# A transformer decoder layer on one core: new order of the opening, and stack rows interleaved over the partitions

## The chip, the cores and the metric

The kernel runs on one core of a Trainium2 chip. The metric is the device time of one execution in microseconds (us).

## The reference

One decoder layer over x of 4 × 512 tokens with 256 numbers each, and a context of 4 × 1024 tokens:

```
x = layernorm(x + attention(x, x, causal))      # 16 heads of 16, scores / sqrt(16), softmax
x = layernorm(x + attention(x, context))        # the same, not causal
x = layernorm(x + moe(x))                       # 8 experts 256 -> 1024 -> 256, gelu, the best 2 of each token
```

Each attention has projections wq, wk, wv, wo of 256 × 256 with biases. All inputs and the output are float32.

## The kernel before, in words

The kernel has two parts. The first (to about 855 us) does both attentions, the norms and the routing; the second does the experts on the tokens sorted by expert, and the last norm. The change touches the first.

**Splits and stacks.** Scores are computed in bf16, yet nearly as exactly as in float32: a projected query or key is split into three bf16 pieces, and the contraction of 16 numbers becomes one of 96: `Q_PART` and `K_PART` say which piece of the query meets which piece of the key in each of six groups of 16 rows. Three further rows hold the row maxima (in three pieces) on the query's side and ones on the key's. One "split" (b, s) makes the pieces for 8 heads and 512 tokens: PE projects (L899, two 512-wide float32 matmuls), ACT writes `rest` and the first piece (L1038, L1039), POOL the second and third (L807 to L811), and SP issues six DMAs (L737) from `parts` (128 partitions, d by h) into the stack (16 rows for each group, 8 heads). Per batch there are ten: 0, 1 queries and 2, 3 keys of the self attention, 4 to 7 keys of the cross attention, 8, 9 its queries. There are two `parts` buffers: ACT starts a split only once the one before last has landed. The self stacks share memory with the experts' weights and are named `stack_or_weights` in the profile; the others are `q_stack_cross` and `k_stack_cross`.

**Units.** A unit is four heads of one batch in one attention: 8 units for the self attentions of batches 0 and 1, then cross and self units in turn. For a unit, "max" multiplies queries by keys on PE (L929, L933, with a mask L934) and DVE reduces the rows (L1101); POOL splits the maxima (L821 to L827), PE turns them (L940), DVE copies them (L1108), and SP writes them to the query stack (L745, `rows_in`). "score" multiplies again with keys as rows (L956, mask L959), ACT takes exp (L1059), "weigh" multiplies by the values (L971). `values` (L912, L1047) are projected in pairs of token tiles. Then come turning and dividing (`o_turn`), `att_turn`, `out`, `stats` and `norm`.

**Order.** `Planner` (L89) simulates the engines with rough costs and writes one list, `ORDER`, at build time. Each engine walks through that list, doing its share in order, with semaphores between the engines; so an instruction that waits holds up all of its engine's later ones. `begin` (L176) puts the loads and constants first and sets the times from which the plan starts.

**The opening before.** SP issues three weights and six bias columns (L704 to L707) under one semaphore, `first_in`, which PE, ACT and DVE each wait for ahead of everything. Then it issues five weights, the router's, two output biases, six norm rows and the router's bias under `const_in`; the projections from the context, the first `out` and the `more_constants` of DVE and POOL wait for all 15. POOL issues x, context and residual (L762 to L772), makes masks, identity and ones (L774 to L800), and waits for `const_in`, before its first split.

Of the kernel before, what the change touches and what calls it, by code (L numbers as in the profile page):

```python
# [75 lines left out]
def key_tiles(kind):  # L76
    return ET if kind else QT
# [8 lines left out]

class Planner:  # L89
# [96 lines left out]
    def needs(self, ev):  # L186
        k, d = ev[0], self.done
        if k == "split":
# [10 lines left out]
            if src is None:  # L199
                return None  # L200
# [84 lines left out]
    def place(self, ev, ready):  # L285
        k, d = ev[0], self.done
        self.order.append(ev)
        if k == "split":
# [6 lines left out]
            done = self.use("pool", high + self.HOP, 2900)  # L295
# [38 lines left out]
        elif k == "weigh":  # L334
# [34 lines left out]
        elif k == "norm":  # L369
            self.held["mv"] = None  # L370
            end = self.use("dve", ready, 1500)
            d["scaled", ev[1], ev[2]] = self.use("pool", end + self.HOP, 4800)
# [121 lines left out]
def decoder_layer(nc, a, out):  # L494
    ctx = ExitStack()
    with ctx:
# [28 lines left out]
        ln_gb = sb("ln_gb", [P, 6, D])  # L525
# [4 lines left out]
        router_b = sb("router_b", [P, E])  # L530
# [7 lines left out]
        first_in = sem("first_in")  # L538
        const_in = sem("const_in")
        const_made = sem("const_made")  # L540
        const_cast = sem("const_cast")
        w_in = [sem("w_in0"), sem("w_in1")]
# [32 lines left out]
        bias = {n: sba("b_" + n, [P, DC]) for n in ("sa_bq", "sa_bk", "sa_bv", "ca_bq", "ca_bk", "ca_bv")}  # L575
        out_b = sba("out_b", [P, 2, D])
# [26 lines left out]
        FIRST_LOADS = 3 + 6  # L603
        N_LOADS = 5 + 1 + 2 + 6 + 1
# [27 lines left out]
        ONE_PAIR = float.fromhex("0x1.007f000000000p+0")  # L632

# [60 lines left out]
        def on_vector(b, kind):  # L694
            return b == B - 1 and kind == 1

        CASTS = 8
# [4 lines left out]
        def _(sp):  # L702
            for n in ("sa_wq", "sa_wk", "sa_wv"):
                sp.dma_start(w[n][:, :, :], a[n].rearrange("(c p) n -> p c n", p=P)).then_inc(first_in, 16)  # L704
            with nc.allow_non_contiguous_dma(reason="six columns of 256 numbers"):
                for n, t in bias.items():
                    sp.dma_start(t[:, :], a[n].rearrange("(c p) -> p c", p=P)).then_inc(first_in, 16)  # L707
# [896 lines left out]
```

## Time and profile before

| | us |
|---|---|
| median of 3 runs | 1187.5 |
| lowest and highest run | 1185.99, 1188.43 |
| the profiled execution | 1185.79 |
| its span in the trace | 1183.9 |

Mean granted TensorE clock of the profiled execution: 0.938 of full speed. The span is the time from the first to the last instruction; the execution adds 1.9 us around it. Busy times of PE (matmul) and PEld (weight load) overlap. "Idle before" is the time in which an engine waited ahead of an instruction, with what released it.

### The profile page before, as it was taken

How to read it: one execution, taken by the hardware profiler on the slowest of the kernel's cores; microseconds unless marked ns; L12 is line 12 of the kernel's file. 1: busy time of each engine (PE TensorE's matmuls, PEld its weight loads, DVE VectorE, ACT ScalarE, POOL GpSimd, SP SyncE). 2: the span in 40 equal slices, each digit the busy share in tenths (PEclk: the TensorE clock that was granted, in tenths of full speed). 3: DMA queues.
4: the chain of work that ended last, by engine and by line, in shares of the span. 5: the costliest groups of instructions: out<-in, count | busy, mean ns of one | idle time of the engine just before them, and what ended most of it. 6: DMA issues, size and time to landing. Idle time of an engine off the chain costs nothing. (4 is left out here: it accounts for less than half of the span.)

```text
span 1183.9 us, 19018 instructions
## 1 busy us (share of the span) xinstructions
PE 1041.1 (88%) x6318; PEld 597.6 (50%) x6319; DVE 558.8 (47%) x905; ACT 588.9 (50%) x1199; POOL 306.5 (26%) x416
## 2 busy tenths in 40 slices
PE   3889889999999998998998998975429999999976
PEld 1544445333335533343432333321329999999965
DVE  2441467775665576665674754740321121111116
ACT  1246344675764575765565665654143334444422
POOL 5533532404105603003223030243021111111104
PEclk8989889999999999999999998996759999999988
DMA  7985466208209304107507042011031203323324
GB/s 191 130 125 81 69 78 75 43 2 100 37 2 132 57 2 62 20 2 105 154 1 81 1 55 27 1 55 54 30 101 53 98 27 111 106 102 115 107 86 141
DMA packets 71069, 83.41 MB, mean 70 GB/s; under 512 B 10592, under 2 KB 64608, under 8 KB 70880
## 3 DMA queue, kind: packets, MB, share of 16 engines
q1 hardware_dynamic: 63328, 63.17, 30.9%
q0 software_dynamic: 5504, 17.34, 4.6%
q10 hardware_dynamic: 2176, 2.10, 0.5%
q8 instruction: 37, 0.61, 0.2%
q14 instruction: 24, 0.20, 0.1%
HBM read 38.63 MB, written 12.10 MB: 43 GB/s over the span
## 5 line engine op out<-in xcount | busy, mean ns | idle before, releaser
L1101 DVE TENSOR_REDUCE max_q<-v_slot 128x1 f32<-128x1024 f32 (+3 forms) x352 | 399.7, 1172 | 185.0 <-PE v_slot L929 121.5
L1059 ACT ACTIVATE probs<-a_bank 128x512 f32<-128x512 f32 (+1 forms) x688 | 362.6, 591 | 219.8 <-PE a_bank L956 139.8
L956 PE MATMUL a_bank<-q_stack_cross,k_stack_cross 99*128 99x512 bf16 x512 | 172.9, 399 | 26.8 <-issue 11.7
L929 PE MATMUL v_slot<-k_stack_cross,q_stack_cross 96*128 96x512 bf16 x512 | 155.7, 390 | 10.0 <-DMA q_stack_cross<-parts 8.8
L1441 ACT ACTIVATE hidden<-a_bank,b 128x128 f32<-128x128 f32 x216 | 79.4, 368 | 153.2 <-PE a_bank L1389 139.2
L971 PE MATMUL o_bank<-probs,v_cross 128*32 128x512 f32 x1024 | 141.9, 627 | 9.2 <-issue 3.8
L956 PEld LDWEIGHTS a_bank<-q_stack_cross,k_stack_cross 99*128 99x128 bf16 x512 | 47.4, 99 | 167.4 <-ACT probs L1059 86.9
L1397 PE MATMUL v_slot<-stack_or_weights,hidden 128*128 128x256 f32 x576 | 130.3, 379 | 0.0
L1397 PEld LDWEIGHTS v_slot<-stack_or_weights,hidden 128*128 128x128 f32 x576 | 106.7, 190 | 13.0
L1389 PE MATMUL a_bank<-x_col,stack_or_weights 128*128 128x128 f32 x864 | 109.6, 277 | 1.6 <-issue 1.6
L1389 PEld LDWEIGHTS a_bank<-x_col,stack_or_weights 128*128 128x128 f32 x864 | 106.3, 194 | 3.8 <-issue 2.0
L1352 POOL DMA_INDIRECT token_out<-y_row,to_i x36 | 34.5, 959 | 241.7 <-DVE y_row L1534 241.7
L821 POOL CAST max_p<-max_q 128x16 bf16<-128x16 f32 x32 | 6.3, 196 | 344.0 <-DVE max_q L1101 343.9
L929 PEld LDWEIGHTS v_slot<-k_stack_cross,q_stack_cross 96*128 96x128 bf16 x512 | 43.9, 100 | 89.8 <-issue 31.7
L807 POOL TENSOR_TENSOR rest<-rest,parts 128x512 f32<-128x512 f32 x40 | 46.2, 1154 | 114.8 <-ACT parts L1039 114.5
L933 PE MATMUL v_slot<-stack_or_weights 96*128 96x128 bf16 (+3 forms) x256 | 62.9, 318 | 8.3 <-issue 4.0
L956 PE MATMUL a_bank<-stack_or_weights 99*128 99x512 bf16 (+3 forms) x256 | 66.5, 317 | 4.2 <-DMA stack_or_weights<-max_t 3.6
L1505 DVE COPY x_col<-v_slot 128x256 f32<-128x256 f32 x37 | 15.7, 424 | 114.0 <-PE v_slot L1376 114.0
L934 PE MATMUL v_slot<-mask_q,ident_b 128*128 128x128 bf16 x256 | 50.9, 228 | 0.0
L959 PE MATMUL a_bank<-mask_k,ident_b 128*128 128x128 bf16 x256 | 50.1, 225 | 0.0
L971 PEld LDWEIGHTS o_bank<-probs,v_cross 128*32 128x32 f32 x1024 | 20.7, 110 | 57.1 <-ACT probs L1059 39.4
L1120 DVE RECIPROCAL recip<-v_slot 128x16 f32<-128x16 f32 x32 | 8.2, 257 | 83.9 <-PE v_slot L979 81.9
(217 smaller groups left out, 1186.1 us busy)
## 6 DMA issues: line engine op xcount, KB each, us to landing
stack_or_weights<-in_e_w SPq DMA_DIRECT2D x16, 1024.0 KB, 7.8
stack_or_weights<-parts SPq DMA_DIRECT2D x96, 128.0 KB, 5.9
k_stack_cross<-parts SPq DMA_DIRECT2D x96, 128.0 KB, 5.9
q_stack_cross<-parts SPq DMA_DIRECT2D x48, 128.0 KB, 6.4
x_slots<-slots_in SPq DMA_DIRECT2D x38, 129.0 KB
ctxt<-in_ctxT POOLq DMA_DIRECT2D x4, 1024.0 KB, 10.6
xt<-in_xT POOLq DMA_DIRECT2D x4, 512.0 KB, 6.8
xres<-in_x POOLq DMA_DIRECT2D x4, 512.0 KB, 4.4
```

Of the source, the lines that this page charges most:

```text
L807: nc.gpsimd.tensor_tensor(rest[i][:, :], rest[i][:, :], parts[i][:, 0, :], ALU.subtract).then_inc(rest_done, 1)
L929: last = nc.tensor.matmul(slot[:, half * S:(half + 1) * S], lhs, k_stack[1][0:KR, G * u + j, half * S:(half + 1) * S], start=True, stop=True)
L933: nc.tensor.matmul(slot[:, at:at + keys], lhs, k_stack[0][0:KR, G * u + j, 0:keys], start=True, stop=False)
L934: last = nc.tensor.matmul(slot[:, at + keys - P:at + keys], ident_b[:, :], mask_q[:, :], start=False, stop=True)
L956: last = nc.tensor.matmul(bank[:, i * cols:(i + 1) * cols], lhs, q_stack[kind][0:KM, G * u + j, q0:S], start=True, stop=bool(kind))
L959: last = nc.tensor.matmul(bank[:, i * cols:i * cols + P], ident_b[:, :], mask_k[:, :], start=False, stop=True)
L971: last = nc.tensor.matmul(o_bank[32 * j:32 * (j + 1), q0:S], v_ext[kind][:, kt, G * u + j, :], probs[NO.tile[n, kt] % 2][:, j, q0:S], star ...
L1059: nc.scalar.activation(probs[tile % 2][:, js[0]:js[-1] + 1, q0:S], a_bank[at % AS][:, 0:len(js) * (S - q0)].rearrange("p (j t) -> p j t", ...
L1101: nc.vector.tensor_reduce(most, rows, X, ALU.max, negate=True).then_inc(v_free, 1)
L1389: last = nc.tensor.matmul(h_bank[f % HB][:, 0:P], w1[i][:, c, f * P:(f + 1) * P], x_col[:, c, :], start=(c == 0), stop=(c == DC - 1))
L1397: last = nc.tensor.matmul(y_bank[:, 0:D], hidden[:, f, :], w2[i][:, f, :], start=(f == 0), stop=(f == FC - 1))
L1441: nc.scalar.activation(hidden[:, f, :], h_bank[f % HB][:, 0:P], ACT.Gelu, bias=b1[:, bass.ds(e * FC + f, 1)]).then_inc(gelu_done, 1)
```

## The change

Seven edits go together:

- x of batch 0 is issued by ACT's queue, each weight gets a semaphore of its own, the six bias columns become one array laid out on the host, and the nine broadcast rows (norms, output biases, router bias) become one DMA. PE, ACT and DVE no longer wait for everything.
- POOL's order at the start becomes constants, context, residual. The constants of the routing and the adding of the residual bias of batch 0 move behind the first unit.
- The ones rows of the cross keys come by one DMA from a small memset of DVE; DVE also makes the ones and zeros of the cross values. ACT has an Exp of one column first.
- The four self splits of batch 0 are made on DVE.
- The first norm (batch 0, self) is made wholly on DVE.
- The planner does not place cross-key splits of batch 0 before the rows of unit 2 are in, and starts its clocks at 6 us.
- Stack rows are interleaved: group g takes rows g, g + 6, g + 12, ... instead of 16 g to 16 g + 15.

```diff
+def on_vector_split(b, s):
+    return b == 0 and s < 4
+def on_vector(b, kind):
+    return (b, kind) in ((0, 0), (B - 1, 1))
...
-        for ev in (("load_x", 0), ("load_ctx", 0), ("load_res", 0), ("constants",), ("more_constants",), ("add_bias", 0)):
+        for ev in (("load_x", 0), ("constants",), ("load_ctx", 0), ("load_res", 0)):
...
-        self.done["load_x", 0], self.done["load_ctx", 0], self.done["load_res", 0] = 12000.0, 16000.0, 18000.0
-        self.free["pe"] = 12000.0
-        self.free["act"] = self.free["dve"] = 13000.0
+        self.done["load_x", 0], self.done["load_ctx", 0], self.done["load_res", 0] = 6000.0, 14000.0, 16000.0
+        self.free["pe"] = self.free["act"] = self.free["dve"] = 6000.0
...
-            if src is None:
+            if src is None or (b == 0 and 4 <= s < 8 and ("rows_in", 2) not in d):
                 return None
...
+            if on_vector_split(*ev[1:]):
+                done = self.use("dve", high + self.HOP, 1800)
+            else:
+                done = self.use("pool", high + self.HOP, 2900)
...
+            if (n, kt) == (0, QT - 1):
+                self.order += [("more_constants",), ("add_bias", 0)]
...
+            if on_vector(*ev[1:]):
+                d["scaled", ev[1], ev[2]] = self.use("dve", 0.0, 2700)
...
+        ONES = 2048
+        ones_wide = probs[1][0:PARTS, :, :].rearrange("p j t -> p (j t)")[:, 0:ONES // 2].bitcast(BF16)
...
         def _(sp):
+            sp.dma_start(w["sa_wq"][:, :, :], a["sa_wq"].rearrange("(c p) n -> p c n", p=P)).then_inc(weight_in["sa_wq"], 16)
+            sp.dma_start(biases[:, :], a["biases"]).then_inc(biases_in, 16)
+            for n in ("sa_wk", "sa_wv", "ca_wk", "ca_wv"):
+                sp.dma_start(w[n][:, :, :], a[n].rearrange("(c p) n -> p c n", p=P)).then_inc(weight_in[n], 16)
+            sp.wait_ge(ones_made, 1)
+            sp.dma_start(k_stack[1][KR:KM, :, :].rearrange("p h t -> p (h t)").rearrange("p (c t) -> p c t", t=ONES),
+                         ones_wide[:, :].unsqueeze(1).to_broadcast([PARTS, H * SE // ONES, ONES])).then_inc(ones_in, 16)
+            sp.dma_start(rows_b[:, :], a["rows"].to_broadcast([P, 8 * D + E])).then_inc(rows_b_in, 16)
+            for n in ("sa_wo", "ca_wq", "ca_wo", "router_w"):
+                target = router_w if n == "router_w" else w[n]
+                sp.dma_start(target[:, :, :], a[n].rearrange("(c p) n -> p c n", p=P)).then_inc(weight_in[n], 16)
...
-                                sp.dma_start(stack[g * HD:(g + 1) * HD, h0:h0 + 8, t0:t0 + S], parts[no % 2][:, part, :]).then_inc(stack_in[s], 16)
+                                sp.dma_start(stack[g:KR:NG, h0:h0 + 8, t0:t0 + S], parts[no % 2][:, part, :]).then_inc(stack_in[s], 16)
...
                 elif k == "more_constants":
-                    pool.wait_ge(const_made, 12)
-                    nc.gpsimd.memset(ones_rows(k_stack[1]), ONE_PAIR).then_inc(const_made, 1)
-                    pool.wait_ge(const_made, 13)
-                    nc.gpsimd.memset(v_ext[1][:, :, :, HD:HD + 1], 1.0).then_inc(const_made, 1)
-                    nc.gpsimd.memset(v_ext[1][:, :, :, HD + 1:], 0.0).then_inc(const_made, 1)
-                    pool.wait_ge(const_in, 16 * N_LOADS)
-                elif k == "split":
+                    pool.wait_ge(rows_b_in, 16)
+                elif k == "split" and not on_vector_split(*ev[1:]):
...
+                    pool.wait_ge(split_done, no)
...
         def _(sc):
-            sc.wait_ge(first_in, 16 * FIRST_LOADS)
+            sc.dma_start(xt[:, :, :], xt_d[:, :, 0:S]).then_inc(xt_first, 16)
+            sc.wait_ge(biases_in, 16)
+            nc.scalar.activation(warm[:, :], biases[:, 0:1], ACT.Exp).then_inc(warmed_up, 1)
...
+                    if js[0] == 0 and tile == 1:
+                        sc.wait_ge(ones_in, 16)
...
         def _(dve):
-            dve.wait_ge(first_in, 16 * FIRST_LOADS)
...
                 elif k == "constants":
+                    nc.vector.memset(ones_wide[:, :].bitcast(F32), ONE_PAIR).then_inc(ones_made, 1)
+                    nc.vector.memset(v_ext[0][:, :, :, HD:HD + 1], 1.0).then_inc(ones_made, 1)
+                    nc.vector.memset(v_ext[0][:, :, :, HD + 1:], 0.0).then_inc(ones_made, 1)
+                    nc.vector.memset(v_ext[1][:, :, :, HD:HD + 1], 1.0).then_inc(ones_made, 1)
+                    nc.vector.memset(v_ext[1][:, :, :, HD + 1:], 0.0).then_inc(ones_made, 1)
+                    nc.vector.memset(ones_rows(k_stack[0]), ONE_PAIR).then_inc(ones_made, 1)
                     dve.wait_ge(const_made, 9)
...
+                elif k == "split" and on_vector_split(*ev[1:]):
+                    no = NO.split[ev]
+                    i = no % 2
+                    dve.wait_ge(a_free, NO.a[ev] + 1)
+                    nc.vector.tensor_tensor(rest[i][:, :], rest[i][:, :], parts[i][:, 0, :], ALU.subtract).then_inc(rest_done, 1)
+                    dve.wait_ge(rest_done, no + 1)
+                    nc.vector.tensor_copy(parts[i][:, 1, :], rest[i][:, :]).then_inc(middle_done, 1)
+                    dve.wait_ge(middle_done, no + 1)
+                    nc.vector.tensor_tensor(parts[i][:, 2, :], rest[i][:, :], parts[i][:, 1, :], ALU.subtract).then_inc(split_done, 1)
```

## Rows read from the trace of the kernel before

**Rows 1.** The page: busy time, share of the span and instructions of each engine.

```profile
PE 1041.1 (88%) x6318; PEld 597.6 (50%) x6319; DVE 558.8 (47%) x905; ACT 588.9 (50%) x1199; POOL 306.5 (26%) x416
```

**Rows 2.** Stretches: us, each engine's busy us (instructions), granted clock, DMA share, GB/s.

```profile
0.00:14.60 14.60, 0.00 (x0) 0.01 (x1) 0.02 (x1) 0.02 (x1) 13.11 (x23) 1.00 0.80 245
0.00:68.80 68.80, 39.47 (x170) 23.70 (x171) 24.68 (x27) 13.90 (x23) 38.72 (x54) 0.94 0.93 158
120.00:160.00 40.00, 33.23 (x208) 19.00 (x207) 22.28 (x36) 12.52 (x23) 20.48 (x26) 0.83 0.56 82
160.00:770.00 610.00, 578.04 (x3413) 242.89 (x3412) 395.18 (x502) 373.19 (x692) 149.99 (x211) 0.97 0.34 48
```

**Rows 3.** Waits of PE over the span: total us, times, longest.

```profile
PE a_bank L899 <- DMA b_ca_bv<-in_ca_bv: 14.7, 1, 14.7
PE a_bank L956 <- issue: 11.7, 3, 8.6
PE a_bank L956 <- DMA q_stack_cross<-max_t: 9.1, 3, 4.7
PE v_slot L929 <- DMA q_stack_cross<-parts: 8.8, 2, 4.6
...
PE a_bank L912 <- DMA router_b<-in_router_b: 5.1, 1, 5.1
...
PE a_bank L956 <- DMA stack_or_weights<-max_t: 3.6, 1, 3.6
...
PE a_bank L912 <- ACT parts L1039: 2.6, 1, 2.6
...
PE a_bank L956 <- ACT parts L1039: 2.5, 3, 1.8
```

**Rows 4.** DMA traffic of 5 to 10 us (loads), and the stretch of 42 to 53 (restacks).

```profile
DMA packets 946, 1.59 MB, mean 318 GB/s; under 512 B 425, under 2 KB 602, under 8 KB 946
...
42.00:53.00 11.00, 10.68 (x61) 7.04 (x62) 6.13 (x7) 3.73 (x6) 4.56 (x9) 1.00 1.15 123
```

**Rows 5.** Line L737, the restack transfers: issue ns min/median/max, and landing.

```profile
L737 SPq DMA_DIRECT2D stack_or_weights<-parts x96: 547/605/1996, 21.1 to 388.6; - x96
...
DMA to landing us min/median/max: 3.2/5.9/12.2
```

**Rows 6.** Timeline, 14 to 31 us: start us, us, engine, line, instruction.

```profile
14.68 3.78 PE L899 MATMUL a_bank<-xt,w_sa_wq 128*128 128x512 f32 x4 [14.68 <-DMA b_ca_bv<-in_ca_bv]
...
16.16 3.47 DVE L1166 MEMSET stack_or_weights<- 3x4096 f32 x1 [0.91 <-issue]
...
18.54 1.28 ACT L1038 ACT_TABLE_LOAD   x1 [18.41 <-PE a_bank L899]
...
19.84 0.69 ACT L1038 ACTIVATE rest<-a_bank,b_sa_bq 128x512 f32<-128x512 f32 x1
...
26.14 2.35 DVE L1172 CAST x_all<-token_i 128x16 f32<-128x16 int32 x1
...
30.32 1.16 POOL L811 TENSOR_TENSOR parts<-rest,parts 128x512 bf16<-128x512 f32 x1
```

**Rows 7.** Landing of x's first two loads; landing of the first weight.

```profile
DMA to landing us min/median/max: 5.7/6.8/7.9
...
w_sa_wq<-in_sa_wq SPq DMA_DIRECT2D x1, 256.0 KB, 2.8
```

**Rows 8.** Groups by shape: DVE (40 to 200 us, 800 to 862 us), PE (420 to 560).

```profile
L1101 DVE TENSOR_REDUCE max_q<-v_slot 128x4 f32<-128x1024 f32 x9 | 11.0, 1224 | 2.1 <-PE v_slot L934 2.1
L1101 DVE TENSOR_REDUCE max_q<-v_slot 128x4 f32<-128x512 f32 x9 | 6.2, 689 | 18.2 <-PE v_slot L934 18.2
...
L1157 DVE TENSOR_TENSOR y_cross<-y_cross,ln_gb 128x1024 f32<-128x1024 f32 x1 | 1.2, 1225 | 0.0
...
L899 PE MATMUL a_bank<-ctxt,w_ca_wk 128*128 128x512 f32 x16 | 7.7, 606 | 0.0
```

**Rows 9.** Timeline: the first row of maxima, copied by DVE.

```profile
52.89 0.21 DVE L1108 COPY max_t<-v_slot 48x128 bf16<-48x128 bf16 x1 [1.85 <-PE v_slot L940]
```

More of the change, by code:

```diff
@@ L371, in place @@
             end = self.use("dve", ready, 1500)
-            d["scaled", ev[1], ev[2]] = self.use("pool", end + self.HOP, 4800)
+            if on_vector(*ev[1:]):
+                d["scaled", ev[1], ev[2]] = self.use("dve", 0.0, 2700)
+            else:
+                d["scaled", ev[1], ev[2]] = self.use("pool", end + self.HOP, 4800)
             d["kept", ev[1], ev[2]] = self.use("pool", 0.0, 2300)
@@ L524, in decoder_layer @@
         ident_b = sb("ident_b", [P, P], BF16)
-        ln_gb = sb("ln_gb", [P, 6, D])
+        rows_b = sb("rows_b", [P, 8 * D + E])
+        ln_gb = rows_b[:, 0:6 * D].rearrange("p (i n) -> p i n", i=6)
+        out_b = rows_b[:, 6 * D:8 * D].rearrange("p (i n) -> p i n", i=2)
+        router_b = rows_b[:, 8 * D:8 * D + E]
         stats = sb("stats", [P, QT, 6])
@@ L574, in decoder_layer @@
         router_w = sba("w_router", [P, DC, E])
-        bias = {n: sba("b_" + n, [P, DC]) for n in ("sa_bq", "sa_bk", "sa_bv", "ca_bq", "ca_bk", "ca_bv")}
-        out_b = sba("out_b", [P, 2, D])
+        biases = sba("biases", [P, 6 * DC])
+        bias = {n: biases[:, DC * i:DC * (i + 1)] for i, n in enumerate(("sa_bq", "sa_bk", "sa_bv", "ca_bq", "ca_bk", "ca_bv"))}
+        warm = sba("warm", [P, 1])
         mask_q = sba("mask_q", [P, P], BF16)
@@ L692, in decoder_layer @@
         early = Routing(xres[:, :, :].rearrange("p q d -> p (q d)"), 0, LAST_BATCH)
-        def on_vector(b, kind):
-            return b == B - 1 and kind == 1
-        CASTS = 8
+        CASTS = 4
         PER_SPLIT = 16 * NG
@@ L757, in _ @@
                 k = ev[0]
-                if k == "load_x":
+                if k == "load_x" and ev[1]:
                     b = ev[1]
@@ L863, in _, with x_there @@
         def _(pe):
-            pe.wait_ge(first_in, 16 * FIRST_LOADS)
+            def x_there(b):
+                if b:
+                    pe.wait_ge(xt_in, 16 * b)
+                else:
+                    pe.wait_ge(xt_first, 16)
             def v_next(ev):
@@ L904, in _ @@
                     src, wname = (ctxt, "ca_wv") if kind else (xt, "sa_wv")
-                    pe.wait_ge(ctx_in if kind else xt_in, 16 * (b + 1))
-                    if kind and b == 0:
-                        pe.wait_ge(const_in, 16 * N_LOADS)
+                    if kind:
+                        pe.wait_ge(ctx_in, 16 * (b + 1))
+                    else:
+                        x_there(b)
+                    if b == 0:
+                        pe.wait_ge(weight_in[wname], 16)
                     bank = a_next(NO.a[ev])
@@ L987, in _ @@
                     pe.wait_ge(a_free, NO.a["att_turn", b, kind] + DC)
-                    if b == 0 and kind == 0:
-                        pe.wait_ge(const_in, 16 * N_LOADS)
+                    if b == 0:
+                        pe.wait_ge(weight_in["ca_wo" if kind else "sa_wo"], 16)
                     slot = v_next(ev)
@@ L1568, in _ @@
             stretch(TT // FT - 1)
-_INS = ["x", "xT", "ctxT"] + [f"{k}_{n}" for k in ("sa", "ca") for n in ("wq", "bq", "wk", "bk", "wv", "bv", "wo", "bo")] + [
-    "ln1_g", "ln1_b", "ln2_g", "ln2_b", "ln3_g", "ln3_b", "router_w", "router_b", "e_w1", "e_b1", "e_w2", "e_b2"]
+_INS = ["x", "xT", "ctxT"] + [f"{k}_{n}" for k in ("sa", "ca") for n in ("wq", "wk", "wv", "wo")] + [
+    "biases", "rows", "router_w", "e_w1", "e_b1", "e_w2", "e_b2"]
 def heads_last(v):
@@ L1591 @@
         given[n] = heads_last(given[n])
+    given["biases"] = _np.stack([given[n].reshape(DC, P) for n in ("sa_bq", "sa_bk", "sa_bv", "ca_bq", "ca_bk", "ca_bv")]).reshape(6 * DC, P).T
+    given["rows"] = _np.concatenate([given[n] for n in ("ln1_g", "ln1_b", "ln2_g", "ln2_b", "ln3_g", "ln3_b", "sa_bo", "ca_bo", "router_b")])[None]
     given["e_b1"] = given["e_b1"].reshape(E, FC, P).transpose(2, 0, 1).reshape(P, E * FC)
```

51 lines of the change are left out of this document (19 added, 32 removed).

## The prediction

> **What bounds the kernel now.** The page's shares come first: TensorE (PE) is busy 88% of the span, the others about half of it or less [rows 1]. The chain of waits names only the second part, from 855 us on: expert matmuls, which the change leaves alone. So I read the attention part by stretches. PE has few holes in its middle (578 us busy of 610 between 160 and 770), but works only 39.5 of the first 68.8 us, up to the first score matmul [rows 2]. PE's order is written out and in order, so I take it that a hole removed ahead of a full PE moves all that follows, experts included. The waits of PE say what the holes are [rows 3]: 14.7 us for the last bias column, 5.1 for the last broadcast row, 3.6 for the first row of maxima; later 9.1 (three times) for rows of maxima, 8.8 (twice) for restacked queries, 2.6 and 2.5 for pieces of a split on ScalarE (ACT).
>
> Behind those later waits stands one resource. A split is six SBUF-to-SBUF transfers of 128 KB into 16 rows each. Such transfers fill the DMA engines (share 1.15) at 123 GB/s, where loads into 128 rows move 318 GB/s [rows 4]. There are 240 of them, landing after 5.9 us in the median [rows 5], and the small rows of maxima share their queue.
>
> **The opening, step by step.** Before, the first matmul starts at 14.7, when the bias columns are in. ACT's table load follows it, 1.3 us. POOL sets memory and then waits for all constants until 26.1, so the first split's last piece starts at 30.3 [rows 6]. The first unit's maxima begin at 42.3, the first score at 68.8.
>
> x and the first weight: x took 5.7 to 7.9 us from issue to landing by POOL's queue, a weight 2.8 [rows 7]. Issued by ACT at about 0.6, x is there at 6.3; bounds 3.5 (landing like the weight) and 10 (like the slowest, with POOL's issue time). The packed biases are one transfer and land by then. The Trainium skill (DMA: Bandwidth & Descriptors, Issuing engines are not separate DMA queues) says that issuing from several engines saves only the sequencer's time, since all run on the same 16 engines; by that x would come near the upper bound. No row here has an ACT issue at the start.
>
> First split: of four matmuls in 3.8 us it needs two, 1.8, then ACT writes twice 0.69 [rows 6]: 9.5 us. The table load lies under x's landing, started by an Exp on a bias. VectorE (DVE) then makes two subtractions of half of 1.22 [rows 8] and a cast of no more: 1.6 taken, 1.8 at most, against about 2.9 on POOL (1.16 for one of its subtractions [rows 6]). Ahead of that DVE has all memsets, with POOL's for the cross values: 3.5 [rows 6], and some 4 for the rest by width, done before 9.5. Cost nothing; without that cover up to 4. SP's new wait, for the wide ones, ends at about 1.5 us, before SP gets there; were it late, the broadcast rows, four loads and all restacks would queue behind it. ACT's wait for those ones, before its second tile, ends some 20 us early.
>
> But the queue is full then. SP puts five weights, the ones, 1 MB of broadcast rows, three more weights and the router's ahead of the first restack. With x, context and residual that is 5.2 MB; at 245 to 318 GB/s from 2 us on [rows 2, 4] it ends at 18 to 23. I take 18, as the 1536 four-byte bias pieces are gone. Two splits are 12 transfers. If the stride of six rows lifts the limit, SP's issue of 0.605 us [rows 5] is the next one: 7.3, so 25.5. If not, 128 KB at 123 GB/s is 1.07: 12.8, so 31. I take the first, by the loads' row. No row has an SBUF-to-SBUF transfer into spread rows, so 1.07 stays the upper bound. The Trainium skill (SBUF — State Buffer, Door 1: The DMA port swizzle) gives 16 adjacent rows 4 of 16 ports, measured at 104 GB/s; by its table the new rows touch 13, two at most on one. This trace's rate for adjacent rows agrees with it.
>
> What is late next is DVE. The fourth split is ahead of the first maxima in the order, and its ACT step waits for the second split's landing: 25.5 + 1.4 + 1.6 = 28.5. The first unit's six reductions, 0.69 + 1.22 + 2 × 0.95 (width between the two) + 2 × 1.22 [rows 8], end at 34.8. Before, 2.1 us passed from there (51.0) to the copied row (53.1 [rows 9]), then 0.8 of issue and a landing; with cross keys held back nothing is in front of it, I take 2.8 as for the weight. First score: 40.5, instead of 68.8.
>
> PE has by then done less: of its 39.5 us, the four cross-key projections (7.7, as for a later batch [rows 8]) and some 5 of the next units' maxima are missing. So 27 of 40.5 busy, idle 13.5 against 29.3: **gain 16**. Bounds: 12 with the old transfer rate, 20 with x at 3.5 and the maxima ahead of the fourth split.
>
> **The rest of the change.** Held-back keys: 24 transfers on SP (14.5 us of issue) and 2.9 a split on POOL now go out while scores run; rows of maxima queue behind at most six, 3.6 us. Two units are ahead by then: cost 0; without that lead 3.6 for each of four, 14. Constants behind the first unit: DVE's cast of 2.35 [rows 6] and three small ones, 3.7 together, where scores keep PE full: 0, at most 3.7. First norm on DVE: three passes of 1.22 instead of three of twice 1.16 on POOL [rows 6, 8]; the cross queries come 3.4 sooner, DVE's maxima behind 3.7 later, and PE idles 6.8 of the 40 us there [rows 2]: 0, between -3 and +3.7. Semaphores for single weights cost nothing, as a wait on an early load ends at once. POOL's wait on the previous split is on one long done.
>
> **Later splits.** The four rows of waits hold 9.1 + 8.8 + 2.6 + 2.5 = 23 us [rows 3]. With transfers at 0.605 instead of 1.07, twelve queued ones clear 5.6 us earlier, more than the longest such wait (4.7). Not all comes back: DVE and ACT, busy 65 and 61% of 160 to 770 [rows 2], catch up during these holes, and the new order makes others. I take less than half, **10**; bounds 0 and 23.
>
> **Sum** against the profiled execution: 1185.8 - 16 - 10 = 1159.8. That execution lies 1.7 below the median of 1187.5; with it I forecast **1161**.
>
> **The rivals.** (a) *The stride changes nothing* (the limit is in the engines or the 1 KB pieces): only the opening gains, 12: 1185.8 - 12 = 1174. For it: no row shows the cure. Against: 318 GB/s with weights in 1 KB and x in 2 KB pieces. (b) *All restack waits go*: 1185.8 - 16 - 23 = 1147. Against it: while PE waits DVE gets ahead, and that lead is lost. (c) *Lost in the next 100 us*: the second batch's self units wait for stacks that the first must have left, and there PE gets only 33 of 40; the gain shrinks to some 6, 1180. (d) *Slower*: the cross keys now cut in between scores. Place: SP's queue, between the rows of maxima of units 2 to 5. Price: at the old rate 4 × 6.4 = 26 us of queue, less 10 of lead, plus the 7.4 of new DVE work there, is 23 against 16 gained: 1193. It decides if a row of maxima lands over 10 us after its copy. Against it: the planner counts SP's time, and the queue is free for units 0 and 1. Beside these, 11.7 us of PE's idle time [rows 3] lie near 800, under the 24 indirect writes, and are given to no releaser but issue; they may change by 8 either way as the writes meet other instructions, which widens every case.
>
> **Chances.** Forecast 0.50, (a) 0.22, (b) 0.13, (c) 0.08, (d) 0.05, and 0.02 for no change. A measurement of this kernel can tell about 0.2% (2.4 us) from nothing. Faster: 0.93; within: 0.02; slower: 0.05. The range, from (b) with a little of the spread near 800 to just short of (c), is 1145 to 1179.
>
> **What would show it.** First matmul at 6 to 7 us; four splits before the first maxima, these from 25 to 29; first score near 40; restack stretches at over 180 GB/s and landings of 3 to 4 us in the median; PE's waits on restacked queries and rows of maxima under 12 together; first expert matmul some 25 earlier, and what follows it as long as before. Restacks still at 120 GB/s would make (a) right; a first score after 50 would say that the loads' queue, not the restacks, sets the opening. Rows of maxima landing late between 45 and 100 would be (d).

## The result, and the profile after

| | before | after |
|---|---|---|
| median, four runs each on one chip | 1187.97 | 1144.47 |
| lowest and highest | 1185.99, 1191.55 | 1142.75, 1147.99 |
| profiled execution, its span | 1185.79, 1183.9 | 1147.99, 1146.3 |
| mean granted clock | 0.938 | 0.952 |

The ratio is 0.9634, with a 95% interval of 0.9602 to 0.9667. The direction was right. The gain of the medians is 43.5 us, where 26.5 was forecast, and the time lies 0.5 under the low end of the range. Which chip these runs had is not known.

The page's busy line, against [rows 1], shows PE with 15 us less of work for the same 6318 matmuls:

```profile
PE 1025.8 (89%) x6318; PEld 592.6 (52%) x6319; DVE 572.4 (50%) x923; ACT 588.8 (51%) x1200; POOL 278.4 (24%) x397
```

The waits of PE over the span, as in [rows 3] (of the matmul lines, L980 is what was L956, L953 what was L929, L957 what was L933, L936 what was L912 and L920 what was L899):

```profile
PE a_bank L980 <- ACT probs L1091: 14.6, 15, 11.4
...
PE a_bank L980 <- issue: 6.4, 2, 6.2
PE a_bank L920 <- DMA xt<-in_xT: 6.2, 1, 6.2
...
PE a_bank L936 <- DMA w_ca_wv<-in_ca_wv: 4.6, 1, 4.6
PE v_slot L957 <- issue: 4.3, 1, 4.3
...
PE a_bank L980 <- DMA stack_or_weights<-max_t: 2.8, 1, 2.8
...
PE a_bank L980 <- ACT parts L1068: 1.1, 2, 0.7
...
PE a_bank L980 <- DMA q_stack_cross<-max_t: 0.3, 1, 0.3
```

No wait on restacked queries is left. The four rows that the prediction added up to 23 us now hold 1.4. The restack transfers, now L757, and their landing, against [rows 5]; and two stretches, in the columns of [rows 2]:

```profile
L757 SPq DMA_DIRECT2D stack_or_weights<-parts x96: 546/600/5163, 11.2 to 373.4; - x96
...
DMA to landing us min/median/max: 2.2/2.4/9.7
```

```profile
21.00:27.00 6.00, 4.05 (x14) 2.28 (x12) 0.00 (x0) 0.00 (x0) 0.00 (x0) 1.00 0.98 203
32.00:36.00 4.00, 4.00 (x17) 3.20 (x17) 2.18 (x3) 0.74 (x2) 0.00 (x0) 0.80 0.73 203
```

The issue of one is as long as before (600 ns), and the median landing fell from 5.9 to 2.4 us. The rate rose from 123 to 203 GB/s. The first of the two stretches still has the last weights in it; the second has restacks alone, and moves 203 GB/s with the DMA engines busy 0.73 of the time instead of 1.15. There SP's issue is the next limit: 128 KB every 0.6 us would be 217 GB/s. The shortest landing fell as well, from 3.2 to 2.2, so a single transfer is faster, and not only a queue of them.

The opening, from the timeline (start, length, engine, line, instruction), against [rows 6, 9]:

```profile
0.83 0.51 ACTq L1043 DMA_DIRECT2D xt<-in_xT  x1
...
11.25 5.16 SPq L757 DMA_DIRECT2D stack_or_weights<-parts  x1
11.26 0.69 DVE L1209 TENSOR_TENSOR rest<-rest,parts 128x512 f32<-128x512 f32 x1 [1.29 <-ACT parts L1068]
...
27.03 0.69 ACT L1067 ACTIVATE rest<-a_bank,biases 128x512 f32<-128x512 f32 x1 [6.67 <-DMA stack_or_weights<-parts]
...
29.26 0.69 ACT L1067 ACTIVATE rest<-a_bank,biases 128x512 f32<-128x512 f32 x1 [0.48 <-DMA stack_or_weights<-parts]
...
29.33 0.22 PE L957 MATMUL v_slot<-stack_or_weights 96*128 96x128 bf16 x1 [4.28 <-issue]
...
32.36 1.82 DVE L1132 TENSOR_REDUCE max_q<-v_slot 128x4 f32<-128x512 f32 x2
...
36.30 0.96 DVE L1132 TENSOR_REDUCE max_q<-v_slot 128x2 f32<-128x768 f32 x1 [2.12 <-PE v_slot L958]
...
44.23 0.22 DVE L1139 COPY max_t<-v_slot 48x128 bf16<-48x128 bf16 x1 [1.58 <-PE v_slot L964]
...
50.12 0.38 PE L980 MATMUL a_bank<-stack_or_weights 99*128 99x512 bf16 x1
```

Of the loads that SP issues ahead of the restacks, the router's is the last to land (issued at 7.47); and x:

```profile
w_router<-in_router_w SPq DMA_DIRECT2D x1, 8.0 KB, 16.6
xt<-in_xT ACTq DMA_DIRECT2D x1, 512.0 KB, 5.3
```

x is in 5.3 us after ACT's issue at 0.83, below the 5.7 to 7.9 of POOL's queue, and the first matmul is at 6.2, forecast 6.3. The loads' queue ends at 24.1, forecast 18. ACT's third split waits for the first split's landing until 27.0, its fourth for the second's until 29.3, forecast 25.5. The 9.6 us by which the first score is late (50.1 for 40.5) then have three parts. DVE's reductions start at 32.4 instead of 28.5, behind the fourth split. They take until 42.65, 10.3 us instead of 6.3, because they wait 4.2 us in all for PE, which the written order has on values matmuls between the maxima (5.1 us at 30.7, then twice 1.9). And from there to the first score it is 7.5 us instead of 5.7: PE does the second unit's maxima first.

**Where the 38 us came from.** The two executions are compared at fixed points of the same work, the starts of ACT's copy of unit n's output:

| unit | before | after | earlier by |
|---|---|---|---|
| 0 | 80.31 | 64.14 | 16.2 |
| 4 | 142.59 | 134.65 | 7.9 |
| 8 | 234.10 | 220.99 | 13.1 |
| 16 | 420.22 | 403.13 | 17.1 |
| 24 | 596.01 | 569.35 | 26.7 |
| 30 | 789.66 | 748.38 | 41.3 |
| 31 | 830.97 | 792.34 | 38.6 |
| end of span | 1183.9 | 1146.3 | 37.6 |

So 13 us are there by unit 8 (PE's idle time is 9.7 less up to there, its busy time 3.4) and 28 come between units 8 and 30. That stretch of the kernel before, and two of its slices:

```profile
234.10:789.66 555.56, 524.00 (x3045) 214.85 (x3044) 354.03 (x452) 342.21 (x634) 129.59 (x189) 0.97 0.32 46
560.00:564.00 4.00, 3.04 (x8) 1.12 (x9) 0.69 (x1) 1.84 (x4) 0.00 (x0) 0.50 1.17 126
564.00:568.00 4.00, 4.00 (x18) 1.03 (x17) 2.32 (x3) 1.76 (x4) 0.00 (x0) 0.71 1.07 242
568.00:572.00 4.00, 3.98 (x22) 1.06 (x19) 4.00 (x4) 2.71 (x6) 0.00 (x0) 1.00 1.08 369
```

And after:

```profile
220.99:748.38 527.39, 513.82 (x3049) 211.09 (x3048) 357.60 (x453) 341.91 (x635) 129.72 (x189) 1.00 0.17 48
```

The same work on PE (the counts differ by 4 of 3045 records) takes 10.2 us less of busy time (524.0 to 513.8), and PE is idle 13.6 us instead of 31.6. Idle 18.0 and busy 10.2 make the 28.2. The busy part is the clock: behind the 4.7 us hole that ends in the slice from 560, the granted clock is 0.50 (the lower of its two levels, 1.2 GHz), then 0.71 as a mean of both, and only then full. One shape of matmul in the kernel before, in the stretches 561 to 566 and 568 to 573:

```profile
L929 PE MATMUL v_slot<-k_stack_cross,q_stack_cross 96*128 96x512 bf16 x4 | 2.1, 634 | 0.0
L929 PE MATMUL v_slot<-k_stack_cross,q_stack_cross 96*128 96x512 bf16 x7 | 2.2, 382 | 0.0
```

The same matmul takes 634 ns behind the hole and 382 a few us later; 382 is also the mean of all 512 of them in the changed kernel. So the hole is paid for twice, and the prediction had only its length.

### The profile page after: what moved, and what is told of

It reads as the page before. It is cut to its first block and busy times, and to the rows that moved or that the text cites. A ratio compares the mean times of both kernels' runs of the same rounds, so it can differ in the third digit from the quotient of the medians.

```text
span 1146.3 us, 19043 instructions
## 1 busy us (share of the span) xinstructions
PE 1025.8 (89%) x6318; PEld 592.6 (52%) x6319; DVE 572.4 (50%) x923; ACT 588.8 (51%) x1200; POOL 278.4 (24%) x397
## 5 line engine op out<-in xcount | busy, mean ns | idle before, releaser
L980 PE MATMUL a_bank<-q_stack_cross,k_stack_cross 99*128 99x512 bf16 x512 | 168.7, 388 | 23.2 <-ACT probs L1091 14.4
L953 PE MATMUL v_slot<-k_stack_cross,q_stack_cross 96*128 96x512 bf16 x512 | 151.9, 382 | 3.9 <-DVE max_q L1132 2.8
L995 PE MATMUL o_bank<-probs,v_cross 128*32 128x512 f32 x1024 | 139.1, 616 | 7.4 <-ACT probs L1091 3.2
L980 PEld LDWEIGHTS a_bank<-q_stack_cross,k_stack_cross 99*128 99x128 bf16 x512 | 46.6, 97 | 157.8 <-ACT probs L1091 101.8
L953 PEld LDWEIGHTS v_slot<-k_stack_cross,q_stack_cross 96*128 96x128 bf16 x512 | 42.7, 98 | 83.8 <-DVE max_q L1132 34.4
L957 PE MATMUL v_slot<-stack_or_weights 96*128 96x128 bf16 (+3 forms) x256 | 62.0, 311 | 8.3 <-issue 4.3
L980 PE MATMUL a_bank<-stack_or_weights 99*128 99x512 bf16 (+3 forms) x256 | 64.9, 309 | 3.4 <-DMA stack_or_weights<-max_t 2.8
L823 POOL TENSOR_TENSOR rest<-rest,parts 128x512 f32<-128x512 f32 x36 | 41.6, 1155 | 99.4 <-ACT parts L1068 98.7
L1067 ACT ACTIVATE rest<-a_bank,biases 128x512 f32<-128x512 f32 x40 | 27.5, 688 | 58.6 <-PE a_bank L920 46.9
```

The lines of the kernel that those rows point to most:

```text
L823: nc.gpsimd.tensor_tensor(rest[i][:, :], rest[i][:, :], parts[i][:, 0, :], ALU.subtract).then_inc(rest_done, 1)
L953: last = nc.tensor.matmul(slot[:, half * S:(half + 1) * S], lhs, k_stack[1][0:KR, G * u + j, half * S:(half + 1) * S], start=True, stop=True)
L957: nc.tensor.matmul(slot[:, at:at + keys], lhs, k_stack[0][0:KR, G * u + j, 0:keys], start=True, stop=False)
L980: last = nc.tensor.matmul(bank[:, i * cols:(i + 1) * cols], lhs, q_stack[kind][0:KM, G * u + j, q0:S], start=True, stop=bool(kind))
L995: last = nc.tensor.matmul(o_bank[32 * j:32 * (j + 1), q0:S], v_ext[kind][:, kt, G * u + j, :], probs[NO.tile[n, kt] % 2][:, j, q0:S], star ...
```

## The experiments

Ratios are to the kernel before on the same chip. There were three chips (A, B, C), on which the kernel before needs 1168.3, 1167.7, and 1185.0 or 1189.1 us (C was used twice). The times expected of the first four runs are for a kernel before of 1188. All edits but those named "before" are to the changed kernel.

### The stride alone, and all but the stride (chip A)

In the changed kernel, rows adjacent again:

```diff
-    sp.dma_start(stack[g:KR:NG, h0:h0 + 8, t0:t0 + S], ...
+    sp.dma_start(stack[g * HD:(g + 1) * HD, h0:h0 + 8, t0:t0 + S], ...
```

> The changed kernel with the stack rows of a group adjacent again (rows 16 g to 16 g + 15), all else kept. Theory 1 (the stride is what was undersized: later restack waits cost over 23 us, more than their idle time): restacks back at 115 to 125 GB/s, landings near 6 us in the median, PE waits on restacked queries and rows of maxima back to some 18 to 23 us after 160 us, time 1144.5 + 30 = 1174 (1168 to 1180), so over two thirds of the gain is the stride. Theory 2 (the opening's new order was undersized and gives most of the 43): 1144.5 + 10 to 15, under 1160. Theory 3 (the two need each other): alone each gives little, here over 1182.

In the kernel before, the same edit the other way round and nothing else:

> The kernel before with only the stack rows interleaved with step 6. Theory 1: the restack waits go, each with the slower clock behind it: 1188 - 27 for the later waits and some 5 in the opening (8 splits' landings), 1156 (1150 to 1162). Theory 2: 1188 - 10, over 1174. Theory 3 (needs the new opening): over 1182. Together with the run of adjacent rows it says if the two parts add up: their gains should sum to 43 within 5 if they do.

| | ratio | interval |
|---|---|---|
| after_adjacent | 1.0005 | 0.9978 to 1.0033 |
| before_stride | 0.9607 | 0.9569 to 0.9645 |

The stride alone gives all of the gain. The whole rest of the change, with adjacent rows, gives nothing. Against a kernel before of 1188 the two ratios are 1188.6 and 1141.3 us: none of the three theories had this, the first expected 1174 and 1156, and the two gains, 0 and 47, do sum to the whole within 5. after_adjacent's landings and PE's waits:

```profile
DMA to landing us min/median/max: 3.2/5.8/12.2
```

```profile
PE v_slot L953 <- DMA q_stack_cross<-parts: 9.7, 2, 5.1
...
PE a_bank L980 <- DMA stack_or_weights<-max_t: 8.2, 3, 6.0
PE v_slot L957 <- issue: 7.5, 2, 5.6
PE a_bank L980 <- DMA q_stack_cross<-max_t: 7.2, 3, 3.1
```

These are much the waits of the kernel before. Unit 0 ends at 67.1, 13 us earlier than in the profile before (another chip, compared only up to unit 30), unit 4 at 144.7 (2 later), unit 8 at 229.0 (5 earlier), unit 30 at 789.2 (0.5 earlier). In before_stride the landings are 2.2/2.4/7.0, no wait on restacked queries is left, and units 8 to 30 take 522.6 us.

### Other strides (chip A)

Steps of two and three rows, in blocks of 32 and 48:

```diff
-    stack[g:KR:NG, ...]
+    stack[32 * (g // 2) + g % 2:32 * (g // 2) + g % 2 + 31:2, ...]
```

```diff
-    stack[g:KR:NG, ...]
+    stack[48 * (g // 3) + g % 3:48 * (g // 3) + g % 3 + 46:3, ...]
```

> The changed kernel with step 2 in place of 6: group g takes every second row of a block of 32. By the port table of the Trainium skill (SBUF - State Buffer, Door 1: The DMA port swizzle) this reaches 8 ports with two rows each, against 13 ports with at most two, and 4 ports with four rows for adjacent rows. Port theory: the fullest port has two rows as with step 6, so restacks run at 190 to 230 GB/s, landings 2.4 to 3.5 us, time within 4 us of the changed kernel (1144 to 1150). Rival (what counts is how far the rows are spread over the 96 rows): a rate between 120 and 180 GB/s and a time near 1155 to 1165.

> The changed kernel with step 3: group g takes every third row of a block of 48. By the same table the fullest port has three of the sixteen rows (for the block 0 to 47). Port theory: slower than step 2 although the rows are spread wider: 145 to 190 GB/s where the queue is full, landings 3 to 4.5 us, time 1147 to 1158. Rival (spread alone counts): faster than or equal to step 2.

The ratios are 0.9634 (0.9595 to 0.9672) and 0.9631 (0.9583 to 0.9679), the median landings 2.5 and 3.1 us, beside 2.4 for six rows and 5.8 for adjacent ones. From 21 to 27 us the rates are 207 and 182 GB/s, beside 203. So the landings came as the port theory had them for both steps, and the longer time that it had for step 3 (1147 to 1158) did not come. Once a landing is down to 3 us, a little more or less of it no longer moves the time: from 32 to 36 us all three steps move 199 to 203 GB/s, the pace of SP's issue, though step 3 needs a DMA share of 1.02 for it and the others 0.72 and 0.73.

The Trainium skill (SBUF — State Buffer, Door 1: The DMA port swizzle) says that the number of ports which a transfer's rows reach sets its rate. By its table adjacent rows reach 4, step 2 reaches 8, step 3 reaches 8 or 12, and step 6 reaches 13 or 14. The trace agrees in that adjacent rows are by far the slowest, but step 3 is slower than step 2 with no fewer ports. What has the order of all four landings is the number of rows on the fullest port by that table: four, then three or two, then two and two. No run varied one of these two counts alone.

### Where the later gain sits (chip C)

The last batch's cross stacks alone on adjacent rows, beside the changed kernel:

```diff
-    stack[g:KR:NG, ...]
+    stack[(slice(g * HD, (g + 1) * HD) if b == B - 1 and s >= 4 else slice(g, KR, NG)), ...]
```

> The changed kernel with adjacent rows for the cross stacks of the last batch alone (s of 4 to 9, b = 3), so the DMA limit returns for six splits of forty. In the kernel before, PE was idle 4.3 + 1.8 + 4.6 = 10.7 us for them. Clock theory (a hole costs its length and, behind it, several us at half clock): from the output of unit 24 to that of unit 30 the stretch grows from 179 to 193 us, 13 to 15 more, with granted clock 0.5 to 0.7 in the 4 to 8 us behind each hole; time 13 to 15 above the changed kernel. Rival (only the idle time counts): 9 to 11 more, clock unchanged.

> The changed kernel itself, for a comparison on one chip with the runs beside it. On the chip of the last four runs the kernel before took 1168 and its stretch from the output of unit 30 to that of unit 31 took 21.8 us in all of them, where the first chip needed 41 to 44. Theory A (the new opening is worth nothing beside the stride): ratio to the kernel before 0.960 to 0.966, as step 2 and the stride alone gave. Theory B (it is worth some 3 us more): 0.957 to 0.959.

The ratios are 0.9775 (0.9747 to 0.9804) and 0.9625 (0.9593 to 0.9657). Up to unit 24 the two agree (565.05 and 564.46). From there to unit 30, first with adjacent rows, then the changed kernel:

```profile
565.05:756.34 191.29, 174.19 (x913) 63.11 (x912) 122.23 (x176) 117.21 (x218) 41.73 (x56) 0.96 0.23 29
612.00:616.00 4.00, 2.04 (x12) 0.34 (x10) 0.00 (x0) 2.07 (x4) 0.00 (x0) 1.00 1.12 120
616.00:620.00 4.00, 0.97 (x3) 0.44 (x4) 0.00 (x0) 0.00 (x0) 0.00 (x0) 0.54 0.35 36
620.00:624.00 4.00, 4.00 (x17) 1.07 (x14) 3.05 (x3) 2.17 (x4) 0.00 (x0) 0.61 0.01 2
```

```profile
564.46:743.54 179.08, 171.84 (x913) 61.72 (x912) 122.04 (x176) 116.79 (x218) 41.67 (x56) 0.99 0.11 31
```

The stretch with its 913 matmuls takes 12.2 us longer: 9.9 idle and 2.35 of busy time. (The medians are 16.6 apart, the two profiled executions 13.8.) The wait row says `PE v_slot L953 <- DMA q_stack_cross<-parts: 9.6, 2, 5.0`, so a wait on a stack comes back at its full length, and behind it the clock is at 0.54 and 0.61. The reason for which the prediction took less than half of such waits, that the other engines get ahead during them, does not hold here.

### Parts of the new opening

Cross keys not held back (chip C):

```diff
-            if src is None or (b == 0 and 4 <= s < 8 and ("rows_in", 2) not in d):
+            if src is None:
```

> The changed kernel without the holding back of the cross keys of batch 0 (the planner may place them as soon as the context is there). If holding them back is what makes the first score early and that counts: first score over 55 us instead of 50, time 3 to 8 longer. If PE's total work up to unit 8 sets the end, the keys merely move: output of unit 7 at the same time within 2 us, time within 3.

Ratio 0.9679 (0.9652 to 0.9706), where the changed kernel beside it has 0.9625. The first score comes at 61.7 and unit 8 ends at 229.3, 12.8 later than in after_again; 11.0 of it is left at unit 30. Holding them back is worth 8 us between the medians (1148.87 and 1140.94), in the upper end of the 3 to 8 expected.

The first norm on GpSimd again (chip B):

```diff
-    return (b, kind) in ((0, 0), (B - 1, 1))
+    return b == B - 1 and kind == 1
```

> The changed kernel with the first norm's three last passes on POOL again, in kernel and planner. Priced at 0 in the prediction, between -3 and +3.7. Expected: output of unit 8 within 3 us of the changed kernel, time within 3 (ratio 0.960 to 0.966).

The first splits on GpSimd again (chip B):

```diff
 def on_vector_split(b, s):
-    return b == 0 and s < 4
+    return False
```

> The changed kernel with the four first splits' pieces made on POOL instead of DVE. The loads' queue theory: the first restacks land with the loads (20 to 27 us) whoever makes the pieces, so the first maxima start within 2 us of 29 and DVE is free for them earlier; time within 3 us of the changed kernel. If making them on DVE counts (1.8 instead of 2.9 each, as forecast), the first score is 2 to 4 later and the time 2 to 4 longer.

And the kernel before with the stride, beside them:

> The kernel before with interleaved rows alone, once more, on whatever chip the changed parts below run on. Theory (the opening's rest adds little beside the stride): ratio to the kernel before 0.960 to 0.966; the changed kernel was 0.9625 and 0.9634 on two chips. If the rest of the change is worth its own 3 us or more, the ratio here is over 0.966.

| chip B | ratio | interval | end of unit 8 |
|---|---|---|---|
| after_norm_pool | 0.9722 | 0.9689 to 0.9755 | 230.14 |
| after_pool_split | 0.957 | 0.9544 to 0.9596 | 216.22 |
| before_stride_again | 0.963 | 0.9606 to 0.9653 | 222.33 |

The norm, priced at -3 to +3.7 and expected within 3 us, is worth far more. Between units 7 and 8, then the same two points in the changed kernel's profile:

```profile
172.12:230.14 58.02, 53.07 (x247) 23.71 (x247) 42.89 (x50) 24.66 (x45) 19.70 (x22) 0.85 0.17 46
```

```profile
181.76:220.99 39.23, 38.60 (x214) 18.25 (x213) 27.20 (x36) 24.53 (x46) 18.84 (x18) 1.00 0.24 69
```

The planner put 33 more matmuls between the points (247 for 214) and the clock there is 0.85. The edit changed the order of everything behind it as well as one engine's work; how much is order and how much the norm itself was not tried. The splits on VectorE gained nothing: without them unit 8 ends where it does in after_again (216.43), and the first score is at 47.4, beside 47.7. If anything they cost: the ratio of after_pool_split lies some 6 to 8 us below the changed kernel's on other chips (0.9625 to 0.9635), where 3 at most was expected. Its profiled execution is the slowest of its four (1122.2, the others 1115.6 to 1118.1), so its trace does not show where that would come from.

The broadcast rows and four late weights behind the first row of maxima in SP's order (chip C):

```diff
-            sp.dma_start(rows_b[:, :], a["rows"].to_broadcast([P, 8 * D + E])).then_inc(rows_b_in, 16)
-            for n in ("sa_wo", "ca_wq", "ca_wo", "router_w"):
...
             for ev in ORDER:
                 k = ev[0]
+                if ev == ("rows_in", 0):
+                    sp.dma_start(rows_b[:, :], a["rows"].to_broadcast([P, 8 * D + E])).then_inc(rows_b_in, 16)
+                    for n in ("sa_wo", "ca_wq", "ca_wo", "router_w"):
...
```

> The changed kernel with the broadcast rows, three weights and the router's issued behind the four first splits instead of ahead of them (1.8 MB). In the changed kernel the first restack was issued at 11.3 us and ACT had to wait for it until 27.0. Theory Q (the loads' queue sets the opening): the restacks land by 20 to 22, maxima begin 5 to 8 us earlier, first score at 42 to 45, output of unit 0 about 5 earlier, and 3 to 6 of it last to the end. Theory W (conserved work): the start is earlier but is given back before unit 8; time within 2 us.

Ratio 0.9603 (0.957 to 0.9636). The first restack's issue takes 0.7 us instead of 5.5, the first two splits have landed by 21.8 and 23.8 instead of 26.4 and 28.6, the maxima start at 24.4 instead of 28.7 and the first score is at 42.4 instead of 47.7. Unit 8 ends 5.2 earlier and unit 30 6.9 earlier. So these loads did delay the first restacks. In the total the median is 3.9 us less than after_again's, with overlapping intervals (0.9593 to 0.9657 there).

### The opening beside the stride, on one chip (chip C), and a faster version

Two kernels again, and one with both of the last findings: the first splits on GpSimd and the five loads behind the first row of maxima.

> The changed kernel again, beside the kernel before with the stride alone, on one chip with five rounds each. So far the two stood on different chips at 0.9634 and 0.9625 (changed) and at 0.9607 and 0.963 (stride alone), so neither of two readings is excluded. Theory A (the opening is spent): what the new opening gains beside the stride, 6 us at the end of unit 0 and again at unit 8, is given back or lost in noise by the last unit; the ratio to the kernel before is 0.962 to 0.965, within 0.002 of the stride alone. Theory B (the opening's gain arrives): the changed kernel is 3 to 7 us ahead of the stride alone at the last unit and in the total, a ratio of 0.957 to 0.960 where the stride alone has 0.963. On the 20 us stretch under the 24 indirect writes (unit 30 to 31): it is 40 to 44 us on a chip where the kernel before needs about 1185, and 21.8 where that needs about 1168.

> The kernel before with the stride of six rows alone. Theory A: ratio 0.961 to 0.964, the same as the whole change on the same chip. Theory B: 0.003 to 0.006 behind the whole change. Both: unit 0 ends 5 to 10 us later than in the whole change; the question is how much of it is left at units 8 and 30. The stretch from unit 30 to 31 has the same length as in the changed kernel on this chip, since it goes by chip and not by kernel.

> The changed kernel with two parts of it undone or moved: the first splits back on GpSimd, and the broadcast rows and the four weights that nothing of the first unit reads issued behind the first row of maxima. Alone the first was worth 6.4 us less time against its chip's kernel before (0.957), the second 2.6 (0.9603). If the two gains are independent the ratio is 0.953 to 0.956, about 9 us better than the changed kernel. If both come from the same stretch (the first unit's start), it is 0.957 to 0.960. If the 0.957 of the splits on GpSimd was spread between chips, as its output milestones (216.2 at unit 8, the changed kernel 216.4) would have it, the ratio is that of the late loads alone, 0.960 to 0.962.

| chip C | median | ratio | interval |
|---|---|---|---|
| after_third | 1145.22 | 0.9635 | 0.9613 to 0.9657 |
| before_stride_third | 1141.17 | 0.9595 | 0.9572 to 0.9618 |
| after_both | 1137.12 | 0.9569 | 0.9547 to 0.9591 |

The changed kernel is not ahead of the stride alone: if anything it is 4 us behind, with intervals that just touch. Up to the end of unit 8, first the changed kernel, then the stride alone, then both findings:

```profile
0.00:219.33 219.33, 191.40 (x1219) 99.80 (x1221) 126.21 (x163) 100.55 (x187) 74.38 (x117) 0.95 0.38 107
```

```profile
0.00:220.41 220.41, 187.69 (x1223) 97.41 (x1225) 115.69 (x147) 100.36 (x186) 102.63 (x136) 0.98 0.40 106
```

```profile
0.00:212.72 212.72, 191.33 (x1219) 99.36 (x1221) 118.92 (x151) 100.96 (x187) 86.07 (x129) 0.95 0.40 111
```

In this pair of traces the new opening saves 4.8 us of PE's idle time (27.9 for 32.7) and pays 3.7 of it in busy time at a lower clock (0.95 for 0.98), for matmuls of the same number within four. It ends unit 0 7.3 us earlier, and then has 463 matmuls to do until unit 4 ends where the stride alone has 418: the held-back keys come due, and unit 4 ends 3.4 later.

One pair of traces can't settle a few us: in the changed kernel's own three traces unit 8 ends at 221.0, 216.4 and 219.3. All traces with spaced rows say it better. In six with the new opening (these three, after_step2, after_step3 and after_scatter_late) unit 8 ends at 218.7 in the mean, in three with the stride alone at 221.6: a lead of 2.9. From unit 8 to 30 the first six need 525.4 to 527.4 us, the other three 522.6 to 524.7, and at unit 30 both means are 745. Here are after_third and before_stride_third in that stretch:

```profile
219.33:744.82 525.49, 512.17 (x3049) 210.84 (x3048) 357.55 (x453) 341.87 (x634) 130.01 (x189) 1.00 0.17 48
220.41:743.04 522.63, 510.51 (x3045) 210.37 (x3044) 355.12 (x452) 341.82 (x635) 129.90 (x189) 1.00 0.17 49
```

So the lead is spent in a stretch that the new opening does not touch directly, by 1.2 us of idle and 1.7 of busy time. Which instructions cost it was not looked for. Of the 3.8 us at the end of the span in this pair, 1.8 are there at unit 30; from 31 on, where the two run the same instructions, the changed kernel takes 2.7 more, 1.9 of it busy time, at a clock of 0.91 for 0.93. Over all traces that part takes 352.3 to 356.1 us (without after_scatter_late), so the 2.7 is within its spread.

after_both has the same busy time up to unit 8 as the changed kernel and 6.5 less idle, reaches the first score at 42.0, is 6.6 earlier at units 8 and 30, and its interval lies below the changed kernel's. It is ahead of the stride alone by 4 us, with overlapping intervals, and has the lowest ratio together with after_pool_split (0.957 on chip B).

### The stretch under the indirect writes

The 24 indirect writes moved to the end of the order (chip B, one run):

```diff
-        self.order.insert(last + 1, ("scatter",))
+        self.order.append(("scatter",))
```

> The changed kernel with the 24 indirect writes of the early scatter moved from behind the last maxima to the end of POOL's first part. On two chips the stretch from the output of unit 30 to that of unit 31 took 41 to 44 us under these writes, PE idle for nothing but issue or ACT, on a third 21.8. If the writes are the cause, the stretch is 21 to 23 us here on any chip (and the experts start later, as the writes now run by themselves for 30 us: time 10 to 20 over the changed kernel). If not, the stretch stays at what the other kernels of this call show.

It took 1149.96 us, a ratio of about 0.985. From unit 30 to 31 it needs 21.8 us, but so does each kernel on chips A and B with its writes in place, so the run says nothing of the cause. The writes then stand alone, and PE has one wait of 28.3 us behind them, where the changed kernel has 2.5.

## Why the prediction was wrong

**The bound and the mechanism: right.** Adjacent rows hold the restacks at 120 to 123 GB/s with the DMA engines full, and the stride lifts that to 203. Rival (a), the stride changes nothing (0.22), and rival (d), slower, fall with before_stride. Rival (c), lost in the next 100 us, describes units 0 to 4 (16.2 earlier, then 7.9), but not the end. Of the signs, the median landing of 2.4 is below the 3 to 4 named, PE's waits on restacked queries and rows of maxima are 3.1 together (under 12 named), and the first expert matmul came 37.8 us earlier (880.11 to 842.28), forecast 25, with what follows it as long as before (304.0 and 303.8).

**The step that failed: "Not all comes back … I take less than half, 10".** It measured 28.2 between units 8 and 30. 18.0 is idle time: the four wait rows fell by 21.6, from 23.0 to 1.4, and only 3.6 came back as other idle time, where the prediction had 13 lost to the lead of DVE and ACT and to the new order. Its own figure, a queue that clears 5.6 us earlier against a longest wait of 4.7, had said that the waits would go. 10.2 is the clock behind each hole, a term that the prediction had nowhere, so that even its upper bound of 23 was too low. after_last_adjacent shows both at once, 9.6 of wait and 2.35 of clock for two holes.

**The opening: 16 forecast, 13 by unit 8, but for another reason.** The first matmul held (6.2 for 6.3). The restacks of two splits came at 29.3 for 25.5, since the loads' queue ended at 24.1 and not at 18 (23 was its upper bound). The first score (50.1 for 40.5) failed by that and by two terms more: "six reductions … end at 34.8" put DVE alone on the path, where PE's order has three stretches of values matmuls between the maxima, and the way from there to the score left out the second unit's maxima. PE was idle 18.5 us up to there, not 13.5. That 13 are there by unit 8 all the same is luck: the stride alone gives 12 by then without any new opening. The lower bound, "12 with the old transfer rate", was not one: at the old rate 5 us were there at unit 8, 0.5 at unit 30, and nothing in the total. Neither with the stride nor without it is the opening worth anything that could be measured in the total.

**The costs set to nothing.** Held-back keys: no cost but a gain, 8 us with the opening as it is, though the work itself came due by unit 4, as above. The norm on DVE: not -3 to +3.7; without it unit 8 ends 9 to 14 us later than in the changed kernel's three traces. First splits on DVE: nothing gained, perhaps something lost. The early loads were in the sum, as a queue that ends at 18; moving five of them gave 5 us by unit 8, and about 4 in the total with intervals that overlap.

**The sum, redone with what was measured.** 1185.8 - 13.1 - 28.2 + 2.7 (unit 30 to 31, 43.96 for 41.31) + 1.0 (after it) = 1148.2, beside 1148.0 profiled. The forecast was 18 short on the later restacks and 3 long on the opening, and had nothing for the last two terms. Rival (b) (0.13) came nearest, 1147 beside 1144.5, and its mechanism, that the restack waits go, is the one seen; but its number is near by luck, with 5 too much of idle time, 3 too much of the opening and nothing of the 10 of clock.

**Shown and not shown.** That the stride makes the gain, and that its later part is waits and the clock behind them, is shown by undoing it alone and doing it alone. Why the opening's milestones are worth so little in the end is only partly shown: the matmuls moved behind unit 0 account for unit 4, and the traces show that the lead left at unit 8 is spent by unit 30, but not by what.

## What to carry to other kernels

Look at which rows a transfer between on-chip buffers lands in, and try to space them, before rearranging anything: a one-line stride was worth 4% here, and a careful new opening nothing that the total shows, with the stride or without it. A hole in a full TensorE was worth its length plus the slow clock behind it, so price both. Where a planner writes the order, a milestone that comes earlier is no gain until the work that was put behind it is counted; compare idle time and busy time up to a point where both kernels have done the same work.

## What the runs showed of the hardware that was not expected

**The clock behind a hole.** After the three holes of 4.3 to 4.7 us in the kernel before, and the two of 4.6 and 5.0 in after_last_adjacent, the granted clock was 0.50 to 0.57 in the slice of 4 us in which PE took up its work again, 0.57 to 0.71 in the next, and 1.00 in the one behind that. For the whole of units 8 to 30 this is 10.2 us against 18.0 more of idle time. The Trainium skill (TensorE: Matmul & The Clock Gate, Part 1: The HAM clock gate (the "warmup" mystery)) says that PE falls to half its clock when it idles and comes back once it is busy again; the slices agree.

**A stretch that goes by chip.** Units 30 to 31, 100 matmuls under the 24 indirect writes, in the changed kernel's profile and in before_stride on chip A:

```profile
748.38:792.34 43.96, 22.25 (x100) 4.31 (x98) 0.68 (x2) 17.44 (x33) 18.10 (x19) 0.69 0.17 61
```

```profile
744.68:766.51 21.83, 18.18 (x100) 4.05 (x98) 0.68 (x2) 17.02 (x34) 16.65 (x18) 1.00 0.30 107
```

On chip C it is 40.6 in the changed kernel, 43.6 when taken again, 44.3 with the stride alone and 42.4 in after_both; on chips A and B 21.8 in each of those looked at. The kernel before differs by about the same amount in its time, 1185 to 1189 against 1168. Of the 11.7 us of [rows 3] that no releaser was found for, 11.4 lie in this stretch, so they seem to go with the chip and not with either kernel; the kernel before was not profiled on A or B. What the slower chips do in it stays open.
